# Two stores of the scan's output move from SyncE's queue to ScalarE's in a four-block convolution and scan kernel

## The reference

```python
x = x + L0(gn(x))   # conv 1x1, 3x3, 1x1 with weights mixed from 8 experts per sample
x = x + L1(gn(x))   # selective scan over the 196 positions, below
x = x + L2(gn(x))   # conv 1x1, deformable conv 3x3, conv 1x1
x = x + L3(gn(x))   # squared convs 1x1, 3x3, 1x1

def L1(x):
    x_ssm, res, gate = split(silu(in_proj(x)))
    xf = silu(depthwise_conv_of_3(x_ssm))
    x_h, dt, B, C = xf and dbc_w @ xf, gathered by perm[head]   # order of the positions, one for each of 2 heads
    y_h = selective_scan(x_h, dt, A, B, C, D)
    y = gather(y_h, argsort(perm))                              # back to the order of the image
    return silu(out_proj(y * silu(gate) + res))
```

## Time and profile before

| What | Value |
|---|---|
| Median of 3 runs | 1047.15 us (1043.2 to 1052.07) |
| The profiled execution's own time | 1048.19 us |
| Its span in the profile | 1046.0 us |
| Mean granted TensorE clock | 0.971 of full speed |
| TensorE busy | 935.8 us, 89% of the span |
| VectorE busy | 731.9 us, 70% |
| ScalarE busy | 550.1 us, 53% |
| GpSimd busy | 362.4 us, 35% |

### The profile page before, as it was taken

The page is one execution under the profiler, slowest core; times in us unless marked ns, Lnnn a source line. Parts: engine busy times, 40 slices in busy tenths (PEclk is TensorE's granted clock), DMA queues, the critical chain, the costliest instruction groups (busy, mean ns, idle before and its releaser), DMA issues.

```text
span 1046.0 us, 19785 instructions
## 1 busy us (share of the span) xinstructions
PE 935.8 (89%) x7460; PEld 635.9 (61%) x7460; DVE 731.9 (70%) x2047; ACT 550.1 (53%) x1155; POOL 362.4 (35%) x320
## 2 busy tenths in 40 slices
PE   3788988999999899999999999999999998887766
PEld 2555656666666566666666666666666665646454
DVE  2567377786878587878878687878787868756332
ACT  1143353756556474748475655657474747361412
POOL 3013433435251625344342525152524343342200
PEclk9889999999999999999999999999999999889998
DMA  9101153352626253544536262626353444426060
GB/s 220 37 8 44 40 141 121 85 177 75 184 75 178 70 169 108 145 128 116 161 94 188 76 190 72 182 79 168 96 164 113 128 130 118 147 64 189 15 207 16
DMA packets 116547, 123.33 MB, mean 118 GB/s; under 512 B 64802, under 2 KB 99750, under 8 KB 116454
## 3 DMA queue, kind: packets, MB, share of 16 engines
q1 hardware_dynamic: 107812, 105.45, 34.6%
q0 software_dynamic: 6144, 13.71, 4.6%
q10 hardware_dynamic: 2498, 2.91, 1.2%
HBM read 84.31 MB, written 37.73 MB: 117 GB/s over the span
## 4 chain that ended last, share of the span: by engine, by line
PE 30%; DVE 24%; issue 17%; POOL 13%; ACT 9%; DMA 5%; SPq 1%; ACTq 0%; POOLq 0%; DVEq 0%
PE ps L625 27%; DVE c_w L1301 4%; ACT y L986 3%; POOL rs L1215 3%; POOL b_ex L1215 3%; POOL b_cr L1215 2%; POOL b_yp L1263 2%; ACT L986 2%; POOL b_res L1215 2%; DVE y L1306 2%; DVE x L1309 2%; DVE st L1336 2%; DMA b_yp<-y_turned,b_to 2%; DVE b_xf L1309 1%; DVE y L1309 1%
## 5 line engine op out<-in xcount | busy, mean ns | idle before, releaser
L1263 POOL DMA_INDIRECT b_yp<-y_turned,b_to x64 | 90.3, 1411 | 271.5 <-DMA y_turned<-b_yt 256.9
L625 PE MATMUL ps<-y,inw 128*128 128x392 f32 x384 | 140.2, 509 | 1.3 <-DVE y L1306 1.3
L1215 POOL TENSOR_TENSOR rs<-ve,root 128x4 f32<-128x4 f32 x64 | 66.1, 1032 | 200.9 <-DVE ve L1305 200.4
L1336 DVE BATCH_NORM_STATS2 st<-x 128x6 f32<-128x196 f32 x256 | 73.7, 350 | 88.0 <-POOL x L1215 76.0
L1301 DVE TENSOR_TENSOR c_w<-c_w,c_hat 126x1176 f32<-126x1176 f32 (+1 forms) x64 | 97.8, 1580 | 11.2 <-DMA c_w<-hat_turned 11.2
L625 PE MATMUL ps<-c_w,c_zt 126*64 126x196 f32 x896 | 88.7, 345 | 11.6 <-DVE c_w L1301 6.9
L625 PEld LDWEIGHTS ps<-y,inw 128*128 128x128 f32 x384 | 70.6, 194 | 46.4 <-issue 6.8
L625 PE MATMUL ps<-w,a_S 128*32 128x384 f32 (+2 forms) x1280 | 81.6, 392 | 7.5 <-DVE a_S L1309 5.7
L625 PE MATMUL ps<-c 128*128 128x256 f32 (+1 forms) x284 | 86.7, 442 | 0.0
L986 ACT ACT_TABLE_LOAD x50 | 64.2, 1283 | 37.5 <-PE ps L625 36.7
L625 PEld LDWEIGHTS ps<-c_w,c_zt 126*64 126x64 f32 x896 | 63.8, 142 | 31.8 <-issue 14.3
(11 more groups left out here) (203 smaller groups left out, 2025.3 us busy)
## 6 DMA issues: line engine op xcount, KB each, us to landing
c_w<-hat_turned SPq DMA_DIRECT2D x32, 771.8 KB
c_w<-hat_turned SPq DMA_DIRECT2D x32, 578.8 KB
z_turned<-c_z SPq DMA_DIRECT2D x32, 441.0 KB
c_zt<-z_turned SPq DMA_DIRECT2D x16, 882.0 KB
b_xp<-x_turned SPq DMA_DIRECT2D x32, 222.0 KB
x<-in_x SPq DMA_DIRECT2D x32, 196.0 KB, 2.7
y_turned<-b_yt SPq DMA_DIRECT2D x32, 196.0 KB
out<-x SPq DMA_DIRECT2D x32, 196.0 KB, 7.3
```

Of the source, the lines that this page charges most:

```text
L625: return nc.tensor.matmul(o, l, r, start=start, stop=stop)
L1215: return nc.gpsimd.tensor_tensor(out=o, in0=x, in1=y, op=op)
L1263: nc.gpsimd.indirect_dma_start(out=YP[:, m, h].rearrange("p b d -> p (b d)"), out_offset=None, in_=y_dram[g % 2], in_offset=bass.IndirectO ...
L1336: last = nc.vector.bn_stats(st[s][:, 2 * c + b, :], x[:, c, b, :])
```

## The change

Step 22 of tb leaves SyncE's list and enters ScalarE's. ScalarE's step 22 has the same two parts, the same waits (for the copy of that half, and, ahead of half 0, for the gathers of group g-2) and the same DMAs. The due time of part 0 is one more than that of step 21, so it comes directly behind ScalarE's copy of half 0. The due time of part 1 is 251000 - 249267 = 1733 above that of step 21; in the list this puts it behind c0 step 7 and s1 step 1 parts 3, 4 and 5 and ahead of s1 step 2, in each group for which those exist (groups 0 to 14; c0 step 7 only to group 13). In group 15 both parts stand directly behind step 21. No other step changes its place in any list.

```diff
 PARTS = {
-    "sync": {... "tb": {22: 2}, ...},
+    "sync": {...},
     "scalar": {...
-               "tb": {0: 1, 3: 1, 9: 1, 10: 2, 20: 1, 21: 1},
+               "tb": {0: 1, 3: 1, 9: 1, 10: 2, 20: 1, 21: 1, 22: 2},
 PLAN, "scalar", tb:
-        (199700, 212014, 238344, 238344, 238344, 245440, 249267),
+        (199700, 212014, 238344, 238344, 238344, 245440, 249267, 249268, 251000),
 PLAN, "sync", tb:
-        (910639, 910639),
+        (),
 ScalarE, tb, behind step 21:
+                if i == 22:
+                    m = part
+                    if m == 0 and g > 1:
+                        for h in range(HEADS):
+                            act.wait_ge(*y_back[h].at(g - 2))
+                    drained(act, ("yt", m), g)
+                    nc.scalar.dma_start(y_dram[g % 2].rearrange("(h t p) x -> t p h x", h=HEADS, t=2)[m],
+                                        YT[:, m].rearrange("p h b d -> p h (b d)")).then_inc(y_out.sem(g), 16)
 SyncE:
-            def tb(i, part, g):
-                m = part
-                if m == 0 and g > 1:
-                    for h in range(HEADS):
-                        sp.wait_ge(*y_back[h].at(g - 2))
-                drained(sp, ("yt", m), g)
-                sp.dma_start(y_dram[g % 2].rearrange("(h t p) x -> t p h x", h=HEADS, t=2)[m],
-                             YT[:, m].rearrange("p h b d -> p h (b d)")).then_inc(y_out.sem(g), 16)
```

More of the change, by code:

```diff
@@ L1847, in once @@
                              a["rows"][0:1, ROW_OFF:ROW_OFF + 2 * TAPS].rearrange("o k -> k o"), ld_d)
-            for_groups("sync", {"n0": n0, "ta": ta, "tb": tb, "f2": f2, "d2": d2, "k3": k3, "once": once})
+            for_groups("sync", {"n0": n0, "ta": ta, "f2": f2, "d2": d2, "k3": k3, "once": once})
             sp.wait_ge(*out_stored.at(GROUPS - 2))
```

## The result

The changed kernel takes 1164.07 us (median of 4 runs, 1160.15 to 1168.88); the kernel before took 1046.18 us beside it. It is 118 us slower. The ratio on record, of the single runs, is 1.1175 with a 95% interval from 1.1126 to 1.1224; the two medians alone divide to 1.1127. The forecast was 1137, the range 1105 to 1175.

A forecast was written before the change was run, and what follows sets the result against it. A path through all engines was taken to set each period, with no slack behind the second store. Stalls 71, clock 20, less 1 for SyncE freed, made 90 us on 1048.19; 1137 us against the median, range 1105 to 1175.

The forecast's parts named there:

- The second store leaves at 570.77, 6.6 us late: Group 8, ScalarE's queue: half 1's store goes after the third in-projection copy ends, where it went at 564.14.
- The gathers start at 573.41 and take 5.2 us: Group 8, GpSimd: four gathers start 2.64 us behind the store's issue, bounds 4.9 and 6.4 us for their length.
- Head 1's transpose is 5.34 us late, 71 us in all: TensorE, group 8: transpose at 580.45 instead of 575.11; the delays of groups 0 to 14 sum to 71 us.
- SyncE freed: SyncE's queue: last c_w quarter and old output's store go sooner; gain of 1 us at the end, bounds 0 and 4.
- Nothing is taken up: Rest of each period: the transposes' delay is passed on in full, as in group 4, whose window was 4.09 us longer.
- The rival that lets later waits shrink: Rival, 5%: VectorE and ScalarE have run ahead, half of 5.2 us is taken up and the clock holds; 1078 us.
- TensorE's clock, 1.7 us in twelve groups, 20 us: TensorE: new stalls lower the granted clock in each group; 1.7 us in twelve groups, bounds 0 and some 3 us.
- group 4's price of 1.2 us: Kernel before, group 4: window 4.09 us longer for a transpose 2.91 us late; the 1.2 us on top taken as clock.
- Group 14's ten windows: Kernel before, group 14: after 3 us of TensorE idle, the 0.50 clock level stood for some ten windows.
- the mark of 65: Window length in us above which the forecast would be wrong, through the clock or another queue.
- clock stays low: Rival, 10%: TensorE stays at the lower clock some ten windows, 5 us a group instead of 1.7; 1177 us.
- freed queue wins: Rival, 4%: without the last c_w quarter beside them, stores, gathers and products are quicker; at most 11.2 us, 1036 us.

The follow-up runs named there:

- the run with half 0 alone: Kernel before with only half 0's store moved to ScalarE's queue, half 1's kept on SyncE's at its old place; 1044.7 us, ratio 0.9997.
- the late store on SyncE: Kernel before, both y stores on SyncE behind c_w quarter and output store, the second also waiting for ScalarE's last in-projection copy; 1167.08 us, ratio 1.1168.
- filler matmuls: Changed kernel plus 9 and 4 matmuls of 128x256 ahead of TensorE's waits for head 0's and head 1's gathers, groups 0 to 14; 1118.62 us, ratio 1.0692.
- the run with both at once: Changed kernel with the second store directly behind the first on ScalarE's queue, ahead of the a_w2 copy; 1115.73 us, ratio 1.0683.
- both runs that only let the quarter and the output store go first: Both stores at once on ScalarE's queue, 1115.73 us, ratio 1.0683; kernel before with both on SyncE behind quarter and output store, 1112.58 us, ratio 1.0682.

## Why the prediction was right, and where it was off

- *The second store leaves at 570.77, 6.6 us late.* Right in place, 0.6 us too much in size: it leaves at 8.14 us of the window against 8.73, so 6.0 us late, because the DMA doesn't wait for the end of the copy ahead of it. Half 0's store costs nothing, as the run with half 0 alone shows.
- *The gathers start at 573.41 and take 5.2 us.* They start at 10.72 us of the window instead of 11.37 and take 6.08 us. Their end was forecast at 16.57 us and came at 16.80. That the two misses cancel was luck for the prediction, which took the gathers to be almost clear of the products. The reason is known only from the late store on SyncE: while the first gather starts beside the last c_w product, its end hangs on that product and not on its start.
- *Head 1's transpose is 5.34 us late, 71 us in all.* Measured 5.58 in group 8 and 74.1 in groups 0 to 14. TensorE's waits of nearly 4 and over 1 us came as 4.02 and 0.85. Some 2.6 of the 74 us aren't the place's but the traffic's, in group 14 (see "SyncE freed" below), so the 71 of the forecast is closer than it looks.
- *Nothing is taken up.* Right within 0.4 us in the ordinary groups. The rival that lets later waits shrink has fallen: with the clock held by filler matmuls the window is 5.4 us longer for a transpose that comes 5.75 us later.
- *TensorE's clock, 1.7 us in twelve groups, 20 us.* This is the term that was mis-sized. It measured 39 us behind the transposes, 3.3 to 3.7 us in the ordinary groups 2, 3 and 5 to 12, which is above the bound of 3 us too; filling the stall gave 39 us back in the windows and 45 by the medians. I had taken group 4's price of 1.2 us and raised it a little. There TensorE waited 2.8 us in all and the lower clock stood for about 3 us; here it waits 4.9 us, and 0.50 stood for some ten, through the transposes, what follows them and nearly all of the out-projection. Group 14's ten windows were the nearer row for a stall of 4 us. A single row was a thin base in any case: in group 5 of the run with both at once, TensorE waits 0.95 and 1.92 us as in that group 4, and there the lower clock stands for nearly 7 us and 2.7 us come behind the transpose. What sets the length besides the wait stays open. The windows, forecast at 62 to 63 us, came at 64.8 for the same reason (65.11 in group 7, just above the mark of 65). The rival "clock stays low" was right in its duration; its price of 5 us a group was too high, and its 1177 us is 13 above the result, where the forecast is 27 below.
- *SyncE freed, a gain of 1 us, bounds 0 and 4.* Wrong in its sign, and for a reason I didn't price: the c_w quarter and the output store behind it go out ahead of the y stores. In groups 3 to 13 of the changed kernel the quarter's packets end at 3.4 to 7.0 us of the window and the output's at 4.9 to 8.4. There this stays hidden, since the late store leaves at 7.9 to 8.2 and the first gather follows 2.6 us behind it. In group 14 the second store leaves at 5.66, these packets last until 9.60, and the first gather starts at 10.82, 5.2 us behind the store. In the run with filler matmuls that group's store also leaves at 5.66, the packets end at 5.84, and the gather starts at 8.25: so some 2.6 us were the traffic's. In group 15, where nothing makes the store late, the first gather starts at 9.96 us instead of 5.76, and from there to the end of the span it is 95.1 us instead of 91.6: 3.5 us lost. The rival "freed queue wins" has the opposite sign too, shown by both runs that only let the quarter and the output store go first (ratios 1.0683 and 1.0682).

Forecast and sum again: 74 + 39 + 3.5 us, less 0.7 us by which the first groups began earlier, is the 116.2 us between the spans, against 71 + 20 - 1.

## What to carry to other kernels

A DMA in an engine's queue leaves when that engine comes to it, so look at what the instructions ahead of it wait for: three short copies, the last waiting for TensorE, made this one 6 us late and the kernel 118 us slower. A waiting DMA in a queue also holds back what stands behind it, and that can be worth keeping: with the y stores no longer ahead of them, a 772 KB load and 392 KB of output went first, and the kernel was 70 us slower in the runs whose y stores weren't late for another reason. When a stall is added ahead of TensorE, price the lower clock by stalls of the same length in the trace, and by several of them, since equal waits were followed by 1.2 us in one run and by 2.7 in another.

## What was not expected of the hardware

- ScalarE issued its DMA at the start of the ACTIVATE ahead of it (both at 629.03), not behind its end 0.59 us later.
- The lower clock stood for some ten us after waits of 4.0 and 0.85 us, though TensorE was busy without a pause for the last eight of them; after waits of 0.9 and 1.9 us it stood for about 3 in group 4 of the kernel before, and for nearly 7 in group 5 of the run with both at once.
- The 196 KB y stores beside the traffic of the c_w quarter and the output store freed the gathers 1.8 to 4.4 us later than in group 8 of the kernel before (groups 3 to 13 of the run with both at once). On the same queue as that traffic it was 1.9 to 4.9 us. The Trainium skill, page "DMA: Bandwidth & Descriptors", section "Issuing engines are not separate DMA queues", says that DMAs run on the same 16 engines and interleave, whichever engine started them; the equal ratios of the two runs agree with it.
- The gather's length depends on VectorE: 0.97 us alone, up to 2.25 us in the changed kernel and 2.59 in the kernel before when it starts beside a c_w product.
